# Attention scores of two heads at a time in the two halves of the TensorE rows, with two-part fp32r operands

## The reference

```python
G = NHEAD // N_KV                                   # 32 heads, 8 key heads, 4 heads in a group
q = bitlinear(x, wq).reshape(B, S, N_KV, G, HEAD_DIM)   # B = 2, S = 512, HEAD_DIM = 8
k = bitlinear(x, wk).reshape(B, S, N_KV, HEAD_DIM)
v = bitlinear(x, wv).reshape(B, S, N_KV, HEAD_DIM)
scores = jnp.einsum('bskgd,btkd->bkgst', q, k) * sm_scale
scores = jnp.where(causal, scores, -jnp.inf)
probs = jax.nn.softmax(scores, axis=-1)
out = jnp.einsum('bkgst,btkd->bskgd', probs, v)
return bitlinear(out.reshape(B, S, D_MODEL), wo)
```

## Time and profile before

| | us |
|---|---|
| median of 3 runs (lowest, highest) | 648.75 (645.51, 650.95) |
| the profiled execution | 644.85 |
| its span | 643.0 |
| TensorE busy | 477.0 (74%) |
| VectorE busy | 419.5 (65%) |
| ScalarE busy | 253.1 (39%) |
| GpSimd busy | 237.2 (37%) |
| mean granted TensorE clock | 0.88 |

### The profile page before, as it was taken

One profiled execution on the slowest core, in us unless ns is written; L12 is line 12 of the kernel. 1 busy time (PEld: TensorE's weight loads), 2 busy tenths in 40 slices (PEclk: granted clock), 3 DMA queues, 4 the chain that ended last, 5 costly groups with the idle time before them and its releaser, 6 DMA issues.

```text
span 643.0 us, 10465 instructions
## 1 busy us (share of the span) xinstructions
PE 477.0 (74%) x2991; PEld 332.3 (52%) x2991; DVE 419.5 (65%) x1090; ACT 253.1 (39%) x493; POOL 237.2 (37%) x337
## 2 busy tenths in 40 slices
PE   0367899999999889798964445695787999989400
PEld 0254545454454357676844334483565778778200
DVE  6898867777786367655498839864614556556284
ACT  1142456665666752325701450424313333333111
POOL 5921224333363822303102211265260555556400
PEclk9996689999999999797987576898897999999855
DMA  6045301011052029500000006983022444443161
GB/s 184 1 125 139 75 21 41 21 36 38 27 163 68 2 90 337 175 0 1 1 1 24 24 25 139 255 240 116 31 108 59 132 127 130 139 122 102 48 239 40
DMA packets 56115, 58.60 MB, mean 91 GB/s; under 512 B 6589, under 2 KB 51718, under 8 KB 56073
## 3 DMA queue, kind: packets, MB, share of 16 engines
q1 hardware_dynamic: 51224, 49.41, 27.9%
q0 software_dynamic: 4848, 8.67, 3.9%
HBM read 36.88 MB, written 25.09 MB: 96 GB/s over the span
## 4 chain that ended last, share of the span: by engine, by line
PE 51%; DVE 24%; issue 9%; ACT 6%; POOL 4%; DMA 2%; another core or an unknown queue 2%; SPq 1%; POOLq 0%; DVEq 0%; ACTq 0%
PE ps L1999 7%; PE ps L1704 7%; PE ps L1833 6%; PE ps L1715 6%; PE ps L2018 4%; PE ps L1764 3%; PE ps L1752 3%; PE ps L1754 3%; DVE st L880 2%; PE ps L1753 2%; PE ps L1989 2%; PE ps L1707 2%; DVE xn L808 2%; DVE hf L1030 2%
## 5 line engine op out<-in xcount | busy, mean ns | idle before, releaser
L974 DVE TENSOR_REDUCE negm<-ps 128x1 f32<-128x512 f32 (+2 forms) x192 | 107.6, 594 | 35.1 <-PE ps L1707 34.3
L1460 ACT ACTIVATE probs<-ps 128x512 f32<-128x512 f32 x160 | 91.6, 597 | 63.5 <-PE ps L1715 62.8
L785 POOL DMA_INDIRECT y_slots_scratch<-yblk,ids x63 | 62.1, 986 | 63.3 <-issue 26.9
L1704 PE MATMUL ps<-k_all,q_all 72*128 (+4 forms) x256 | 72.5, 324 | 10.7 <-DMA q_all<-q_parts_scratch 8.8
L1715 PE MATMUL ps<-q_all,k_all 75*128 (+4 forms) x256 | 64.9, 316 | 2.9 <-ACT probs L1460 2.3
L625 POOL TENSOR_TENSOR rstd<-ve,halfneg 128x4 f32<-128x4 f32 x16 | 16.4, 1024 | 129.9 <-DVE ve L911 84.3
L1999 PE MATMUL ps<-wgu,xcol 128*128 x252 | 58.3, 355 | 3.4 <-issue 1.8
L1707 PE MATMUL ps<-hide_cols,identb 128*128 128x128 bf16 x256 | 54.1, 231 | 0.0
L1704 PEld LDWEIGHTS ps<-k_all,q_all 72*128 72x128 bf16 (+1 forms) x256 | 25.6, 103 | 51.2 <-issue 33.4
L1833 PE MATMUL ps<-probs,v_now 128*32 128x128 f32 (+3 forms) x512 | 47.8, 450 | 0.7 <-DVE att L999 0.7
L1999 PEld LDWEIGHTS ps<-wgu,xcol 128*128 128x128 f32 x252 | 40.3, 193 | 12.2 <-issue 9.5
(11 more groups left out here) (288 smaller groups left out, 1163.8 us busy)
## 6 DMA issues: line engine op xcount, KB each, us to landing
x_sorted_scratch<-pad SPq DMA_DIRECT2D x7, 1206.0 KB, 14.3
xblk<-x_sorted_scratch SPq DMA_DIRECT2D x63, 134.0 KB
wgu<-in_moe_w SPq DMA_DIRECT2D x4, 1536.0 KB
q_all<-q_parts_scratch SPq DMA_DIRECT2D x48, 96.0 KB
ycomb<-y_slots_scratch SPq DMA_DIRECT2D x8, 512.0 KB, 4.4
wd<-in_moe_w SPq DMA_DIRECT2D x1, 3072.0 KB, 18.6
sraw<-in_moe_w SPq DMA_DIRECT2D x6, 384.0 KB, 3.4
q_parts_scratch<-qparts SPq DMA_DIRECT2D x6, 256.0 KB, 2.5
```

The costliest lines, as they stand in the source:

```text
L785: pool.indirect_dma_start(out=y_slots, out_offset=bass.IndirectOffsetOnAxis(ap=ids[:, i:i + 1], axis=0), in_=yblk[:, i % YR, :], in_offset ...
L974: dve.tensor_reduce(negm[:, par, qt, h0:h0 + nh], ps[:, u % 4, 0:nh * w].rearrange("p (h t) -> p h t", h=nh), AX.X, ALU.max, negate=True). ...
L1460: act.activation(probs[:, par, u, :], ps[:, 4 + u % 2, :], ACT.Exp)\
L1704: pe.matmul(ps[:, u % 4, c:c + w], q_all[0:72, bass.ds(g * (GQ * T) + (h * T + qt * P), P)], k_all[0:72, bass.ds(g * T, w)], start=True, s ...
```

## The change

Queries and keys are split into two fp32r parts (high by ScalarE, low by one VectorE subtraction from the bank). The four products of parts with 8 features make 32 contraction rows; row 32 is a row of ones (keys) against zero (queries), rows 33 and 34 carry the two parts of the negative maximum. The even heads of a group lie on partitions 0 to 34, the odd heads on 64 to 98, and the matmuls of two heads are issued in turn, one for each half of the rows, into different banks. The mask is added with half identities of 64 rows, so it takes two matmuls a head. Row units are pairs of banks: 6 a group, reduced over both banks by one instruction, with four banks as two pairs. Column units come in pairs, 5 a group, in three rotating banks (4, 5, 6). The maxima are transposed by VectorE in blocks of 32 by 32 and go through DRAM: four writes, a wait, two reads. Queries live in a ring of four groups; the ring is zeroed at the start and rows of ones are loaded. The values of an even and an odd group stand in different columns of their 32-column strips, so two groups accumulate in bank 7 and are copied, transposed and divided together in odd slots. The value products move to units 1, 2 and 3. The copy of the values of a group (`v_now`) goes. The loop is written out as 20 slots.

```diff
-        UNITS = ([(3, h, 1) for h in range(4)] + [(2, h, 1) for h in range(4)]
-                 + [(1, 0, 2), (1, 2, 2), (0, 0, 2), (0, 2, 2)])
-        MT_AT, MROW_AT, OT_AT, DIV_AT, PV_AT, OC_AT = 3, 4, 1, 3, 7, 9
+        ROWS = [(3, 0, 1), (3, 1, 1), (2, 0, 1), (2, 1, 1), (1, 0, 2), (0, 0, 2)]
+        COLS = [[(0, 0, 0)], [(0, 1, 0)], [(1, 0, 0), (3, 0, 384)], [(1, 1, 0), (3, 1, 384)],
+                [(2, 0, 0), (2, 1, 256)]]
+        MT_AT, DIV_AT, OT_AT, OC_AT = 1, 0, 0, 9
+        PV_AT = {1: [0], 2: [1], 3: [2, 3]}
+        def lane(rg, rows):
+            return slice(64 * rg, 64 * rg + rows)
+        def col_unit(g, u):
+            return 4 + (2 * CU * g + u) % 3
...
@@ sync: load_k, four loads, and load_q, four loads from a ring of four groups
+                for rg in range(2):
+                    for j in range(2):
+                        sp.dma_start(
+                            q_ring[64 * rg + 16 * j:64 * rg + 16 * j + 16, g % QRING, :, :]
+                            .bitcast(F32), heads[rg]).then_inc(q_in[g % 2], 16)
@@ sync: slot n
+                if 3 <= n + 1 < NG:
+                    load_q(n + 1)
                 if has(n, 1):
                     g = n - 1
-                    need(sp, mrow_ready, g + 1)
-                    for i in range(3):
-                        sp.dma_start(q_all[72 + i:73 + i, ...], mrow[...])
+                    sp.wait_ge(mt_ready, g + 1)
+                    for k in range(4):
+                        sp.dma_start(places[k], m_cols[32 * k:32 * k + 32, g % 2, :])\
+                            .then_inc(m_out[g % 2], 16)
+                    sp.wait_ge(m_out[g % 2], 64 * (g // 2 + 1))
+                    for rg in range(2):
+                        sp.dma_start(q_ring[64 * rg + MAX_AT:64 * rg + MAX_AT + 2, g % QRING, :, :]
+                            .bitcast(F32), m_dram[g, rg]...).then_inc(m_in[g % 2], 16)
@@ gpsimd: slot n, two steps for the maxima, not four, in their old place ahead of the last hide
@@ vector: slot n
+                        pair_of = ps[:, u % 2 * 2:u % 2 * 2 + 2, 0:nh * w]
+                            dve.tensor_reduce(negm[:, par, :, hp, qt], pair_of, AX.X, ALU.max,
+                                              negate=True).then_inc(s1_read, 1)
-                    if u == 2 and has(n, 2):
-                        dve.tensor_scalar(v_now[...], v_all[...], 1.0, None, ALU.mult)
+                    if u == MT_AT and has(n, 1):
+                        dve.wait_ge(msplit, g + 1)
+                        dve.transpose(m_cols[:, g % 2, :], m3[...]).then_inc(mt_ready, 1)
+                    if u == DIV_AT and has(n, 4) and n % 2:
+                        (one reciprocal, two multiplications, for two groups)
@@ tensor
+            def score_rows(g, u):
+                need(pe, s1_read, RU * g + u - 1)
+                for h in range(nh):
+                    for rg in range(2):
+                        pe.matmul(ps[:, u % 2 * 2 + rg, end - w:end],
+                                  q_ring[lane(rg, KP + 1), g % QRING, h0 + h, qt * P:(qt + 1) * P],
+                                  k_all[lane(rg, KP + 1), g * T:g * T + w], start=True, stop=False)
+                    for rg in range(2):   (mask, the rows 64 * rg of the block: 128 columns)
+                    for rg in range(2):   (mask, the other 64 rows: 64 columns)
+            def score_cols(g, p):
+                if p == 0:
+                    pe.wait_ge(m_in[g % 2], 32 * (g // 2 + 1))
+                need(pe, st_exp, 2 * (CU * g + p) - 1)
+            def weighted(g, kt):
+                if kt == 0:
+                    need(pe, att_ready, g // 2 * 2)
+                    pe.wait_ge(hidden, 4 * (g + 1))
+                for u in range(RU):
                     if has(n, 0):
+                        score_rows(n, u)
+                    if u == OT_AT and has(n, 4) and n % 2:
+                        out_rows(n - 4)
+                    if has(n, 2) and u < CU:
+                        score_cols(n - 2, u)
+                    if has(n, 3) and u in PV_AT:
+                        for kt in PV_AT[u]:
+                            weighted(n - 3, kt)
```

More of the change, by code:

```diff
@@ L465, in spill @@
                 sp.wait_ge(k_split, b + 1)
-                for i in range(3):
+                for i in range(2):
                     rows_i = slice(i * NKV * HD, (i + 1) * NKV * HD)
@@ L505, in slot @@
+            sp.wait_ge(s_ready, 3)
+            for g in range(3):
+                load_q(g)
             def slot(n, par, pair):
+                if n == 0:
+                    spill(1)
+                if n == 1:
+                    load_k(1)
+                if n == FIRST - 1:
+                    sp.wait_ge(q_spilled, 32 * B)
+                if 3 <= n + 1 < NG:
+                    load_q(n + 1)
                 if has(n, 1):
                     g = n - 1
-                    need(sp, mrow_ready, g + 1)
@@ L618, in _ @@
             pool.dma_start(hide_cols[:], consts[:, P:2 * P]).then_inc(s_constb, 16)
+            for half in range(2):
+                here, there = slice(64 * half, 64 * half + 64), slice(64 - 64 * half, P - 64 * half)
+                pool.dma_start(swapped[here, :], consts[there, 0:P]).then_inc(s_constb, 16)
+                pool.dma_start(hide_swap[here, :], consts[there, P:2 * P]).then_inc(s_constb, 16)
             def power(n):
@@ L634, in _ @@
             chain.settle()
-            pool.memset(v_all[:, :].rearrange("p (a c) -> p a c", c=32)[:, :, HD:HD + 1],
-                        1.0).then_inc(s_ready, 1)
-            pool.wait_ge(s_ready, 4)
+            for odd in range(2):
+                pool.memset(v_all[:, :].rearrange("p (g two a c) -> p two g a c", two=2, a=TPB, c=32)
+                            [:, odd, :, :, 16 * odd + HD:16 * odd + HD + 1], 1.0)\
+                    .then_inc(s_ready, 1)
+            pool.wait_ge(s_ready, 5)
             pool.wait_ge(s_w2, 32)
@@ L714, in slot @@
                                            ALU.subtract).then_inc(w13_lo, 1)
-                if isinstance(n, int) and n == NG + 1:
+                if n == NG + 1:
                     power(3)
             late_constants()
-            slots(chain, slot, 12)
+            slots(slot)
             power(4)
@@ L1009, in slot @@
-                if isinstance(n, int) and n == NG:
+                        for two in range(2):
+                            at = (g - 1 + two) % 4 * 32
+                            dve.tensor_tensor(
+                                att4[:, g // 4 * TPB:(g // 4 + 1) * TPB, at:at + 32]
+                                .rearrange("p s (h d) -> p s h d", h=GQ),
+                                o4[:, :, :, two, 0:HD],
+                                rsum[:, :, :, two].unsqueeze(3).to_broadcast((P, TPB, GQ, HD)),
+                                ALU.mult).then_inc(att_ready, 1)
@@ L1017, in _ @@
             att4 = att[:, :].rearrange("p (g s c) -> p (g s) c", s=TPB, c=4 * 32)
-            slots(chain, slot, 2)
+            slots(slot)
             split_low(1, 0)
@@ L1453, in slot @@
             def slot(n, par, pair):
-                for u in range(10):
+                for u in range(2 * CU):
                     if has(n, 2):
@@ L1481, in slot @@
                     act.copy(hi[:, :, :], raw[:, :, :]).then_inc(w13_hi, 1)
-                if isinstance(n, int) and n == NG:
+                if n == NG:
                     split_high(0, 0)
-            slots(act, slot)
+            slots(slot)
             split_high(1, 0)
@@ L1861, in mlp_down @@
                 mm.then_inc(down_done, 1)
-            slots(pe, slot)
+            slots(slot)
             pe.wait_ge(att_ready, NG)
```

404 lines of the change are left out of this document (182 added, 222 removed).

## The result

The changed kernel took 709.97 us (708.54 to 711.06, 4 runs) beside 649.40 (645.51 to 650.95) of the kernel before: a ratio of 1.094 [1.090, 1.098], 9% slower. The forecast was 638, its range ended at 662. The profiled execution has a span of 709.3 us (before 643.0).

A forecast was written before the change was run, and what follows sets the result against it. TensorE was taken to bound the steady attention loop. Terms -3.0 + 0.3 - 1.5 - 5.1 - 1.5 = -10.8 took the profiled 644.85 us to 634.0, in medians 638; the range was 622 to 662.

The forecast's parts named there:

- the steady slots: Attention loop, slots 5 to 15: 9.35 us each in place of 9.82, 5.1 us saved over 11 slots.
- case D: Rival: TensorE's clock falls between a slot's last value product and the next's first; 2.3 us a slot, up to 670; chance 0.18.
- Before the first scores: Start of the kernel: query split ends 3.4 us earlier, 0.4 given back for loads, gain 3.0.
- the term of 0.4 for the longer loads: Before the first scores: longer spill and loads, four in place of three, priced as one more issue, 0.4 us.
- Slots 0 to 4: Early loop: slots 0 and 1 cost 0.3 us in all, slots 2 to 4 save 1.5.
- Halves together: TensorE in a slot: at the lower end both row halves run wholly together, 512 columns taking 0.23 us.
- P: Stretch from a slot's first value product to the slot's end: 6.2 us, from 5.1 to 7.3.
- Wait (1): Column scores wait for maxima through DRAM; column scores' start to the next at least 8.35 us, setting the even slot.
- L: Time for maxima through DRAM, four writes, a wait, two reads: 6.0 us, from 5 to 8.
- case A: Rival: halves cost only their streams; 8.6 us a slot, about 20 us off, 628.5; chance 0.25.
- B: The forecast itself: steady slots of 9.35 us, 638 us in all; chance 0.33.
- The end of the attention: The 24.6 us after the last row scores, exponentials alternating with GpSimd's weight splits: 1.5 us off.

The follow-up runs named there:

- e1: Changed kernel with 62 (score rows) and 64 (column scores) contracted rows per half, wait for the ones moved ahead of the scores: 644.96 us, ratio 0.993.
- e14: Changed kernel, rows narrow, with its value products in units 1, 2, 4 and 5: 707.83 us, ratio 1.092.
- e4: Changed kernel with only TensorE's wait for the rows of ones moved to ahead of the scores: 706.63 us, ratio 1.090.
- e5: e1 with 46 and 48 contracted rows per half in place of 62 and 64: 641.44 us on another chip, ratio 1.020.
- e13: e1 with the score rows back at 33 per half, column scores left at 64: 661.93 us, ratio 1.022.
- e10: e9 with the first group's keys loaded alone, second batch's spills in slots 1 and 2, its key load spread over slots 3 to 6: 631.80 us, 0.975.
- e11: e10 with the fourth block of value products in unit 4 in place of unit 3: 627.00 us, ratio 0.965.
- e9: e1 run again unchanged, as base on the same chip for later versions: 642.05 us, ratio 0.990.
- e2: Changed kernel, rows narrow, plus 24 dense matmuls of 128 rows and 512 columns once, ahead of slot 4: 708.27 us, ratio 1.093.
- e3: Changed kernel, rows narrow, plus one dense matmul ahead of each row unit in slots 2 to 15: two runs, 670.46 and 771.14 us, no ratio.
- e6: e1 with the first group's keys loaded alone, second batch's spill in slot 1 and key load in slot 4: 624.28 us on e5's chip, ratio 0.993.

## Why the prediction was wrong

**The step that failed** is the steady slots, "9.35 each, for 9.82", a gain of "11 x 0.47 = 5.1 us": it priced all of TensorE's work at full clock. Measured 13.9 us a slot at half clock in place of 9.35. e1, with the same columns in the same order, took 8.8 at full clock. So the clock is the whole error of that step and more. From the maxima of group 2 to those of group 14 the changed kernel takes 166.7 us and e1 107.8: 58.9 of the 66.2 by which their spans differ. (The first slots of e1 are at half clock too, 0.52 from 70 to 90 us.)

**The clue was in case D, which had a chance of 0.18 and the wrong place and price.**
- The evidence. The earlier trace rows showed score products of 72 and 75 rows at half clock while TensorE was busy all the time. I counted it against D that full clock was held later "in every slot with dense scores between value products" and that slots 16 and 17 kept it while standing. But the change replaces just these scores by ones of 33 and 35 rows in a half. The trace of before could not vouch for a mix that it does not contain. Standing was not the danger: in e1 TensorE stands 2.2 of 20 us at 1.00.
- The place. D looked at the stretch without value products. e14 shortens it and changes nothing; e1 beside e4, e5 and e13 move rows alone and the clock follows.
- The price. I took 2.3 us a slot from a few cold rows and so ended at 670. At half clock the value products alone are 1.86 + 1.44 + 1.44 (151.44 - 150.00, third and fourth block together) = 4.74 us a slot against 1.00 + 0.78 + 0.79 = 2.57 in e1, 2.2 more. TensorE's whole work of a slot is 13.7 us against 7.7, so scores, masks and transposes have 3.8 more; 0.9 of standing goes, which leaves the 5.1. A price for the clock has to double every stream of the slot.

TensorE was busy for 19.7 of 20 us at half clock after the change, and for 17.8 of 20 us at full clock in e1. The Trainium skill, TensorE: Matmul & The Clock Gate, section Part 1: The HAM clock gate, says that the clock is set by how busy TensorE has been. Taken as the busy time of the profile, that would give the changed kernel the full clock and about e1's time; the runs do not agree, and the measurement decides.

**Before the first scores: -3.0 forecast, +4.3 measured.** The query spill did start earlier, at 39.44 (before 41.20). What was wrong is the term of 0.4 for the longer loads. The query load issued at 44.38 is used at 55.62, 11.2 us later, where the earlier trace rows has 4.65 from issue to landing: the loads of all keys stand ahead of it, on more bytes, and land from 46.8 to 53.6, two microseconds apart. e10 and e11, with one group's keys ahead, start the scores at 46.7 and 46.2. The ones cost up to 1 us by the forecast and 1.6 by e4.

**Slots 0 to 4: +0.3 and -1.5 forecast, -0.6 at full clock.** From the first scores to the maxima of group 3 the kernel before takes 43.6 us and e1 43.0. In the changed kernel it is 46.4, with the clock at half.

**Slots at full clock (read in e1).** Halves together: right, and nearer the lower end. A 512-wide pair is 0.24 us from start to mask, the 0.23 that the earlier trace rows has for one product:

```profile
147.25 0.42 PE L1724 MATMUL ps<-k_all,q_ring 62*128 62x512 f32 x2
147.49 0.23 PE L1730 MATMUL ps<-hide_cols,identb 64*128 64x128 bf16 x1
...
148.61 1.06 PE L1766 MATMUL ps<-probs,v_all 128*32 128x512 f32 x8
...
154.97 0.50 PE L1724 MATMUL ps<-k_all,q_ring 62*128 62x512 f32 x2 [0.69 <-DVE negm L994]
...
157.37 0.50 PE L1745 MATMUL ps<-q_ring,k_all 64*128 64x512 f32 x2 [0.41 <-ACT probs L1476]
157.80 1.07 PE L1766 MATMUL ps<-probs,v_all 128*32 128x512 f32 x8
```

P, from 148.61 to the last mask's end at 154.28, is 5.7 us (forecast 6.2, range 5.1 to 7.3). Entering a value product costs 0.19 beyond the 0.24 of the pair ahead of it (157.37 to 157.80; forecast 0.15). In an odd slot the value product starts 2.83 us in (157.80 - 154.97; forecast 3.35). VectorE's reductions 1.22 and 0.96 and its transpose 0.20, ScalarE's 0.595: right.

Wait (1), which was to set the even slots, does not bind. The maxima of an odd slot, their reads, and the even slot's column scores, which wait for nothing:

```profile
158.74 0.20 DVE L1004 STREAM_TRANSPOSE m_cols<-m 128x32 f32<-128x32 f32 x1
...
161.70 0.53 SPq L538 DMA_DIRECT2D q_ring<-max_parts_scratch  x2
...
164.56 0.51 PE L1745 MATMUL ps<-q_ring,k_all 64*128 64x512 f32 x2
```

The last read is issued 3.5 us after the transpose's start here and in 11 of the 16 groups (3.6 at most), up to 5.0 in the other steady ones. Where TensorE did stand for the maxima, the first time, it went on 1.3 us after the last issue (75.11 after 73.82). That makes L an estimated 4.8 us, forecast 6.0, and the column scores come 5.8 us after that start. TensorE waits instead for an exponential (0.41 above) and, ahead of each slot's first scores, for VectorE's read of a unit before (0.69), which the forecast does not have. Added up, an odd slot is 2.8 + 5.7 + 0.7 = 9.2 and an even one 2.1 + 5.7 + 0.7 = 8.5. By time, 8.8 a slot, the changed kernel at full clock is near case A (8.6), not B (9.35), though A too let the maxima set the even slot.

**The end of the attention: -1.5 forecast, +9.4 measured** (32.0 against 22.6 us between its two marks). It is not the loop's clock alone, because e1 has +10.7 there and gives back nearly all of the 12.9 that its loop gained. The chain at that place, of e1, then of the kernel before:

```profile
217.20 6.27 issue
223.51 1.02 POOL rstd L647
...
227.51 4.50 PE ps L1766 x32
```

```profile
222.92 1.15 issue
224.10 1.03 POOL rstd L625
...
229.75 0.30 DVE att L999
230.10 2.36 PE ps L1833 x32
```

In both kernels the last zeroing of future keys stands in GpSimd's queue behind a step of the next normalization, and that waits for the output projection of batch 0. (In the kernel before, VectorE's division, behind the same normalization, ends 1 us later still and releases the value products.) In e1 that step comes at 223.51, hardly sooner than before (224.10), though the scores were 10.6 us ahead. The clock had fallen to 0.62 to 0.69 between 200 and 220 us, where before it was 1.00, and the last value products took 4.50 for 2.36:

```profile
215.00:220.00 5.00, 5.00 (x29) 1.75 (x28) 0.00 (x0) 2.32 (x5) 2.20 (x1) 0.62 0.01 3
```

How much of the 10.7 is this clock and how much the queue order was not separated: no run changed the tail alone. The runs give an idea of it. Between the two marks e1 takes 33.3 us at a mean clock of 0.69, e9 and e10 32.1 at 0.73, the changed kernel 32.0 at 0.74, e11 30.4 at 0.83, and the kernel before 22.6 at 1.00. Drawn on in a straight line to 1.00 the first ones come to an estimated 27, so some 6 of the 10.7 would be the clock and 4 the rest.

**What stays open.** The two halves together hold 66 to 70 rows at once, hardly fewer than the 72 and 75 before, and yet the clock fell. Whether it is the halves, the fp32r type or the shorter time of dense columns in a slot that makes the difference was not tried. Nor was it tried whether rows of zeros in both operands would do; the added rows are always ones in the keys. That more rows bring the clock back, zeros or not, is shown (e1, e9), as is a state in between at 46 and 48 rows (e5) and with one kind widened (e13).

## What to carry to other kernels

When a change makes TensorE's operands thinner, ask first what clock the thinner mix will be granted, and price the other case by doubling every stream of the slot; the old trace can't vouch for a mix that it lacks. Where rows are free, fill them: contracting over zeros up to the full half cost no time here and was worth 61.7 us. And when a loop gets shorter, look for the step behind it that waits for something else, and for the loads in front of it that now stand ahead of small, urgent transfers.

## What the runs showed of the hardware

- The granted clock follows the rows that products contract over, even where one operand's added rows are all zero: 0.50 in the loop at 33 and 35 rows a half (e4), between both levels at 46 and 48 (e5), 1.00 at 62 and 64 (e1, e9), with the same columns.
- Dense matmuls can raise the clock (0.50 to 1.00 in e2), and the narrow mix behind them lost it again within two slots. With one of them ahead of every row unit, a profiled run held 1.00 from 110 to 210 us (e3).
- Contracted rows cost no time: 0.49 us for a pair of 33 rows and 512 columns (e2), 0.50 for 62 rows (e1), both at full clock.
- Chips differ: the kernel before took 650.02, 649.67 and 647.84 us in three sets of runs and 630.15 in a fourth, on another chip. Its lead lies behind the attention (388.8 us in e6 to 408.8 in e1); the steady slots take the same. The ratios of the experiments are each to the runs of the same chip.
